# One-core fp32 attention-and-experts block: the router's logits from one packed stationary block of gate parts, and the last batch's logits from four column groups

## The reference, cut to what matters

```python
x = x + tanh(g_xattn[0]) * attention(_layernorm(x), ctx_512, W_k, b_k, ln_gamma, ln_beta)   # softmax of normalised scores
h = _layernorm(x)                        # 2048 tokens x 512
logits = h @ gate_w                      # 2048 x 32: one logit for each token and expert
scores = sigmoid(logits)
sfc = scores + e_bias                    # picks 2 of 4 groups, then 4 of 32 experts
...
routed = einsum('tei,te,eih->th', relu2(einsum('th,ehi->tei', h, Wu)), combine, Wd)
shared = relu2(h @ Wsu) @ Wsd
x = x + tanh(g_ffn[0]) * (routed + shared)
```

## Time and profile before

| | |
|---|---|
| median of 3 runs | 559.65 us |
| lowest and highest run | 558.96 and 562.34 us |
| span of the profiled execution | 550.4 us |
| what lies around the span (lowest run less span) | 8.56 us; to the median it is 9.25 us |
| TensorE matmul busy | 538.5 us (98%) |
| TensorE weight load busy | 440.5 us (80%) |
| VectorE busy | 411.3 us (75%) |
| ScalarE busy | 339.2 us (62%) |
| GpSimd busy | 194.7 us (35%) |
| granted TensorE clock | full (9 of 9 tenths in all 40 slices) |

### The profile page before, as it was taken

One profiled execution on the slowest core, in us unless ns is written; L12 is line 12 of the kernel. 1 busy time (PEld: TensorE's weight loads), 2 busy tenths in 40 slices (PEclk: granted clock), 3 DMA queues, 4 the chain that ended last, 5 costly groups with the idle time before them and its releaser, 6 DMA issues.

```text
span 550.4 us, 11107 instructions
## 1 busy us (share of the span) xinstructions
PE 538.5 (98%) x3079; PEld 440.5 (80%) x3079; DVE 411.3 (75%) x906; ACT 339.2 (62%) x670; POOL 194.7 (35%) x197
## 2 busy tenths in 40 slices
PE   7989999999999999999999999999999999999997
PEld 4547786788688878999999999999998889987553
DVE  5699994494868958656778897777667665756997
ACT  4769573755235855667678787776766766763210
POOL 3110100000000024555656766666666656522000
PEclk9999999999999999999999999999999999999999
DMA  8930102006000006997877988787887778899998
GB/s 316 357 117 23 65 14 76 2 1 229 2 1 0 2 21 197 316 333 247 290 249 254 300 276 261 272 269 263 285 292 265 246 247 262 293 308 386 413 414 302
DMA packets 56393, 116.48 MB, mean 212 GB/s; under 512 B 5493, under 2 KB 24054, under 8 KB 55926
## 3 DMA queue, kind: packets, MB, share of 16 engines
q1 hardware_dynamic: 43200, 72.97, 39.7%
q0 software_dynamic: 12960, 42.48, 21.1%
q10 hardware_dynamic: 150, 0.07, 0.0%
HBM read 85.87 MB, written 29.62 MB: 210 GB/s over the span
## 4 chain that ended last, share of the span: by engine, by line
PE 88%; DVE 7%; ACT 2%; issue 1%; DMA 1%; another core or an unknown queue 0%; ACTq 0%; DVEq 0%; POOLq 0%
PE U L1809 38%; PE D L1809 37%; PE T L2167 6%; PE D L2186 3%; PE T L1809 2%; PE T L1968 1%; DVE X L1135 1%; DVE bst L1140 1%; DVE PS L1123 1%; DVE PS L1117 1%; DMA xg<-h_rows,idx_g 1%; DVE bst L1094 1%; DMA wk<-in_L_xattn_W_k 1%; DVE wsd_lo L1177 0%
## 5 line engine op out<-in xcount | busy, mean ns | idle before, releaser
L621 POOL DMA_INDIRECT xg<-h_rows,idx_g x81 | 88.2, 1089 | 107.9 <-DVE tab L1537 76.7
L628 POOL DMA_INDIRECT y_rows<-yb,idx_s x81 | 92.0, 1136 | 85.1 <-issue 46.9
L1568 DVE TENSOR_TENSOR xgT_lo<-T,xgT_hi 128x512 fp32r<-128x512 f32 x81 | 55.9, 690 | 45.2 <-ACT xgT_hi L923 44.1
L940 ACT ACTIVATE yb<-D 128x512 f32<-128x512 f32 x81 | 48.5, 598 | 53.4 <-PE D L1809 52.1
L1809 PE MATMUL U<-wu_hi,xgT_hi 128*128 x324 | 58.6, 302 | 1.5 <-DVE xgT_lo L1568 1.4
L1809 PE MATMUL D<-wd_hi,eaT_hi 128*128 x162 | 57.3, 435 | 0.1
L923 ACT ACTIVATE xgT_hi<-T 128x512 fp32r<-128x512 f32 x81 | 48.2, 595 | 9.8 <-issue 7.4
L1809 PE MATMUL U<-wu_hi,xgT_lo 128*128 x324 | 51.9, 282 | 0.0
L1809 PE MATMUL U<-wu_lo,xgT_hi 128*128 x324 | 51.7, 281 | 0.0
L1573 DVE SCALAR_TENSOR_TENSOR eact<-U,erel 128x256 f32<-128x256 f32 x81 | 34.0, 419 | 22.5 <-issue 11.7
L1809 PE MATMUL D<-wd_lo,eaT_hi 128*128 x162 | 50.6, 394 | 0.0
(11 more groups left out here) (268 smaller groups left out, 1174.5 us busy)
## 6 DMA issues: line engine op xcount, KB each, us to landing
wu<-in_L_ffn_Wu SPq DMA_DIRECT2D x32, 512.0 KB
wd<-in_L_ffn_Wd SPq DMA_DIRECT2D x32, 512.0 KB
yg<-y_rows SPq DMA_DIRECT2D x18, 512.0 KB, 11.7
out<-X SPq DMA_DIRECT2D x16, 256.0 KB, 5.6
X<-in_x SPq DMA_DIRECT2D x3, 1024.0 KB, 11.0
h_rows<-HR SPq DMA_DIRECT2D x3, 1024.0 KB, 4.3
yg<-y_rows SPq DMA_DIRECT2D x3, 1024.0 KB, 12.9
wsu<-in_L_ffn_Wsu SPq DMA_DIRECT2D x2, 1024.0 KB, 7.3
```

Source lines behind the costliest of these rows:

```text
L621: pool.indirect_dma_start(out=xg[:, u, :], out_offset=None, in_=h_dram[:, :], in_offset=bass.IndirectOffsetOnAxis(ap=idx_g[:, t:t + 1], ax ...
L628: pool.indirect_dma_start(out=y_dram[:, :], in_=yb[:, u, :], in_offset=None, out_offset=bass.IndirectOffsetOnAxis(ap=idx_s[:, t:t + 1], ax ...
L940: ac.activation(yb[:, t % UNROLL, :], D[2 + t % 2][:, :], ACT.Copy)\
L1568: ve.tensor_tensor(xgT_lo[:, t % 2, :, :], T[t % 2][:, :].rearrange("p (h n) -> p h n", h=HB), xgT_hi[:, t % 2, :, :].bitcast(f32), ALU.su ...
```

## The change

For batches 0 to 2 the gates' high part (columns 0 to 31) and low part (columns 32 to 63) stand in one stationary block gate_hl, and `logits_t` runs 8 matmuls: gate_hl by hT_hi and gate_hl by hT_lo. The bank then holds two partial sums on 64 partitions (the product of the two low parts, left out before, is in it). For batch 3 the four fp32 matmuls write four different groups of 32 partitions, each complete in itself, in place of summing into one. ScalarE copies 64 or 128 partitions to lgT, TensorE turns 64 or 128 rows a tile, and VectorE sums the 2 or 4 parts with a tensor_reduce (256 or 512 elements in, 128 out) where it copied. GpSimd writes one block of zeros of 128x256 in place of two of 128x384, and the counts that wait for it go from 22 to 21. In VectorE's list `scaled(1, 3)` moves from behind `low_part(1)` to ahead of `low_part(0)`. The tile `spare` keeps the addresses.

```diff
--- before.py
+++ after.py
@@ -65,7 +65,7 @@
         ebias = sb("ebias", [P, E])
         with ExitStack() as chosen_all:
             wsu_h4 = chosen_all.enter_context(nc.sbuf_tensor("wsu_h4", [P, 2, HB, P], f32r))
-        lgT = sb("lgT", [E, SEQ])
+        lgT = sb("lgT", [P, SEQ])
         LG = sb("LG", [P, NT, E])
         LG2 = LG[:, :, :].rearrange("p t e -> p (t e)")
         bst = sb("bst", [P, 2, TPB, 6])
@@ -129,8 +129,8 @@
             hT_lo = at("hT_lo", [P, 2, HB, SEQ], front, f32r)
             wsu_hi = at("wsu_hi", [P, HB, SI], front, f32r)
             wsd_hi = at("wsd_hi", [P, SB, H], front, f32r)
-            gate_hi = at("gate_hi", [P, HB, P], front, f32r)
-            gate_lo = at("gate_lo", [P, HB, P], front, f32r)
+            gate_hl = at("gate_hl", [P, HB, P], front, f32r)
+            spare = at("spare", [P, HB, P], front)
             act_hi = at("act_hi", [P, A_SLOTS, SEQ], front, f32r)
             with ExitStack() as whole:
                 wsu = at("wsu", [P, HB, SI], whole)
@@ -293,6 +293,10 @@
 
             return U[0 if g else 1]
 
+        def logit_rows(b):
+
+            return HB * E if b == N_BATCH - 1 else 2 * E
+
         def keys_of(b):
 
             return key2[:, b, :] if b < 2 else keyT[:, :]
@@ -581,9 +585,8 @@
             pool.tensor_scalar(part_s[:, :], part_i[:, :], float(P), 0.0, ALU.mult, ALU.add).then_inc(c, 1)
             pool.tensor_copy(tok_f[:, :], tok_i[:, :]).then_inc(c, 1)
             pool.wait_ge(s["pool_c"], 14)
-            same = iota_f[:, E:P].unsqueeze(1).broadcast_to([P, HB, P - E])
-            for part in (gate_hi, gate_lo):
-                pool.tensor_tensor(part[:, :, E:P], same, same, ALU.subtract).then_inc(c, 1)
+            same = iota_f[:, 2 * E:P].unsqueeze(1).broadcast_to([P, HB, P - 2 * E])
+            pool.tensor_tensor(gate_hl[:, :, 2 * E:P], same, same, ALU.subtract).then_inc(c, 1)
             pool.tensor_copy(spare_f[:, :], spare_i[:, :]).then_inc(c, 1)
 
             def roots(j, n):
@@ -598,8 +601,8 @@
             roots(1, 2)
             roots(0, 3)
             pool.wait_ge(s["act_gt"], 1)
-            pool.tensor_tensor(gate_lo[:, :, 0:E], gate[:, :, :],
-                              gate_hi[:, :, 0:E].bitcast(f32), ALU.subtract).then_inc(s["pool_gt"], 1)
+            pool.tensor_tensor(gate_hl[:, :, E:2 * E], gate[:, :, :],
+                              gate_hl[:, :, 0:E].bitcast(f32), ALU.subtract).then_inc(s["pool_gt"], 1)
             roots(1, 4)
             for b in range(2, N_BATCH):
                 roots(0, 2 * b + 1)
@@ -751,7 +754,8 @@
                 ac.wait_ge(s["pe_lgT"], b + 1)
                 if b:
                     ac.wait_ge(s["pe_lg"], b)
-                ac.activation(lgT[:, :], U[1][0:E, :], ACT.Copy).then_inc(s["act_lgT"], 1)
+                n = logit_rows(b)
+                ac.activation(lgT[0:n, :], U[1][0:n, :], ACT.Copy).then_inc(s["act_lgT"], 1)
 
             def high_part(j):
                 ac.wait_ge(d_ws[j], 16)
@@ -803,7 +807,7 @@
             h_t(0, 2)
             h_t(0, 3)
             ac.wait_ge(s["d_gate"], 16 * 2)
-            ac.activation(gate_hi[:, :, 0:E], gate[:, :, :], ACT.Copy).then_inc(s["act_gt"], 1)
+            ac.activation(gate_hl[:, :, 0:E], gate[:, :, :], ACT.Copy).then_inc(s["act_gt"], 1)
             high_part(2)
             exps(1, 0)
             relu2(0)
@@ -1161,7 +1165,9 @@
 
             def logits(b):
                 ve.wait_ge(s["pe_lg"], b + 1)
-                ve.tensor_copy(LG2[:, b * TPB * E:(b + 1) * TPB * E], U[1][:, 0:TPB * E]).then_inc(s["dve_lg"], 1)
+                n = logit_rows(b)
+                parts = U[1][:, 0:TPB * n].rearrange("p (t h e) -> p t e h", t=TPB, e=E)
+                ve.tensor_reduce(LG[:, b * TPB:(b + 1) * TPB, :], parts, AX.X, ALU.add).then_inc(s["dve_lg"], 1)
 
             def high_weights(j):
 
@@ -1200,7 +1206,7 @@
             score_spread(0)
             x_part(1, 0)
             x_part(1, 1)
-            ve.wait_ge(s["pool_c"], 22)
+            ve.wait_ge(s["pool_c"], 21)
             scaled(0, 0)
             scaled(0, 1)
             shifted(0, 0)
@@ -1237,6 +1243,7 @@
             shifted(1, 1)
             low_weights(2)
             low_weights(3)
+            scaled(1, 3)
             low_part(0)
             added(1, 0)
             added(1, 1)
@@ -1245,7 +1252,6 @@
             x2_part(1, 1)
             shifted(1, 2)
             low_part(1)
-            scaled(1, 3)
             added(1, 2)
             shifted(1, 3)
             x2_part(1, 2)
@@ -1974,8 +1980,8 @@
                     pe.wait_ge(s["act_tT"], TPB)
                     pe.wait_ge(s["dve_lg"], b)
                     for h in range(HB):
-                        i_ = mm(U[1][0:E, :].rearrange("p (t n) -> p t n", n=P), gate[:, h, :],
-                                HR[:, :, h * P:(h + 1) * P], h == 0, h == HB - 1)
+                        i_ = mm(U[1][h * E:(h + 1) * E, :].rearrange("p (t n) -> p t n", n=P), gate[:, h, :],
+                                HR[:, :, h * P:(h + 1) * P])
                     i_.then_inc(s["pe_lgT"], 1)
                     return
                 pe.wait_ge(s["act_hT"], TPB * b + TPB)
@@ -1987,17 +1993,17 @@
                 else:
                     pe.wait_ge(s["act_outT"], 4)
                 pe.wait_ge(s["dve_hT"], TPB * b + TPB)
-                gates, hs = (gate_hi, gate_lo), (hT_hi, hT_lo)
-                for a, b_ in ((0, 0), (1, 0), (0, 1)):
+                for part in (hT_hi, hT_lo):
                     for h in range(HB):
-                        i_ = mm(U[1][:, :], gates[a][:, h, :], hs[b_][:, b % 2, h, :], a == b_ == 0 and h == 0,
-                                b_ == 1 and h == HB - 1)
+                        i_ = mm(U[1][:, :], gate_hl[:, h, :], part[:, b % 2, h, :], part is hT_hi and h == 0,
+                                part is hT_lo and h == HB - 1)
                 i_.then_inc(s["pe_lgT"], 1)
 
             def logits(b):
                 pe.wait_ge(s["act_lgT"], b + 1)
+                n = logit_rows(b)
                 for it in range(TPB):
-                    i_ = pe.transpose(U[1][:, it * E:(it + 1) * E], lgT[:, it * P:(it + 1) * P], ident[0:E, 0:E])
+                    i_ = pe.transpose(U[1][:, it * n:(it + 1) * n], lgT[0:n, it * P:(it + 1) * P], ident[0:n, 0:n])
                 i_.then_inc(s["pe_lg"], 1)
 
             ctx_t(0)
@@ -2114,7 +2120,7 @@
             down_shared(12)
             up_shared(15)
             down_shared(13)
-            pe.wait_ge(s["pool_c"], 22)
+            pe.wait_ge(s["pool_c"], 21)
             pe.wait_ge(s["dve_c"], 2)
             pe.wait_ge(s["dve_M"], 2)
             ch = chosen[:, :, :].rearrange("p e t -> p (e t)")
```

## The result

| | kernel before | kernel after |
|---|---|---|
| median | 559.44 us | 556.24 us |
| lowest to highest, 20 runs each | 554.53 to 564.52 us | 553.13 to 559.35 us |
| span of the profiled execution | 550.4 us | 554.3 us |
| first gathered tile on TensorE | 206.52 us | 202.37 us |
| from there to the end of the span | 343.88 us | 351.93 us |

The forecast was 556.5 us. The profiled execution of the changed kernel is nevertheless 3.9 us longer than the one of before. The two lower lines of the table say where that comes from: everything up to the first gathered tile is 4.15 us shorter, and the expert stage of this one execution is 8 us longer. The two halves have to be read apart.

The account below looks back on a forecast made before the run. TensorE was taken as full from 57.3 us on, with the chain through VectorE before that. The terms 0.1 + 1.84 + 1.29 - 0.1 = 3.1 us, off 559.65, gave 556.5 us, range 554.6 to 558.6.

Parts of the forecast that it names:

- Batch 3's products: Batch 3's logits on TensorE: five pass times in place of eight, 1.29 us gained.
- rival 2: Batch 3's logits: all four products run side by side, 2.58 us gained there, 555.2 us in all; chance 0.20.
- Batches 1 and 2: Their logits on TensorE, where it is full: four matmuls fewer in each batch, 1.84 us gained.
- Batch 0 and the move: Up to `ctx_t(3)`: a 0.74 us lead at `down_shared(0)` mostly lost to VectorE's third `h_low`; 0.1 us gained.
- Turning back: TensorE's transposes of the logits: twelve tiles with more rows cost at most 0.2 us, 0.1 taken.
- The sums on VectorE: tensor_reduce in place of the copy: 0.42 and 0.70 us, +0.14 and +0.42, hidden by VectorE's idle time and room.
- The sum over the front: All terms together: 3.1 us gained, with the first gathered tile about 3.1 us earlier.
- What lies around the span: Time outside the profiled span: 9.25 us to the median, taken to stay the same.
- runs as before: Expert stage: starts earlier, with the distance from the first gathered tile to the end the same.
- I am wrong if that distance grows: Test for the expert stage: the distance from the first gathered tile to the end should stay the same.
- rival 3: Expert stage: the weight stream falls behind, 0.85 us a stall, up to 8.8 us slower, 568.5 us; chance 0.05.

Follow-up runs that it names:

- kernel 5: Changed kernel with batch 3's four products in two column groups, alternating 0, 1, 0, 1, two products summed in each; 546.25 us, ratio 0.9936.
- kernel 6: Changed kernel with batch 3's four products in two column groups, in blocks 0, 0, 1, 1, two products summed in each; 546.58 us, ratio 0.9936.
- Kernel 1: Kernel before with only the packing of batches 0 to 2; batch 3 and VectorE's order as before; 552.73 us, ratio 0.9987.
- kernel 3: Changed kernel with `scaled(1, 3)` put back behind `low_part(1)`; 548.04 us, ratio 0.9921.
- Kernel 8: Changed kernel with `scaled(1, 3)` ahead of `low_part(1)`, `shifted(2, 0)` behind batch 1's third `h_low`, and `shifted(2, 1)` ahead of `added(2, 0)`; 545.09 us, ratio 0.9930.
- Kernel 4: Changed kernel with only the counter of two VectorE waits in the expert stage cut to six bits; 549.75 us, ratio 0.9936.
- kernel 9: Kernel before with only the counter of two VectorE waits in the expert stage cut to six bits; 559.86 us, ratio 1.0053.
- kernel 7: Changed kernel with batch 1's eight logit matmuls run eight times over, 56 matmuls more; 558.07 us, ratio 1.0154.
- kernels 1 and 2: The second: kernel before with only batch 3's four products in four column groups, summed by tensor_reduce; 550.11 us, ratio 0.9950.
- 9 to 11: The last two: changed kernel with only the cut wait counter, 551.55 us, ratio 0.9826; the other VectorE order again, 549.42 us, ratio 0.9799.

## Why the prediction was right, and where it was not

The time, 556.5 us, was met by 0.3 us. That it came so close is luck: the front became 4.2 us shorter, not 3.1, and the scatter of the expert stage, or something given back there, hid the surplus.

1. **Batch 3's products: wrong, 1.29 us forecast, 2.56 measured** (3.55 - 0.99). This is the step that failed, and what happened is rival 2, which had a chance of 0.20 beside the forecast's 0.45. The reason given was: "passes start in the order of the list, so the second pass waits for the first. The first pass of the next product can start beside the second of this one, but its own second cannot." Kernels 5 and 6 refute it: by that rule they need 2.25 and 3.1 us, and they took 1.84 and 1.85. A second pass has to wait only within its own group. Four groups of two passes make 2 pass times, two groups of four make 4, one group of eight makes 8. The rule of the Trainium skill (TensorE: Matmul & The Clock Gate, Part 3) that matmuls of different column groups run beside one another held, for products of two passes too. The Trainium skill's other rule in that part, that a weight load overlaps a running matmul only where the row group differs, did not: all eight loads, on the same 128 rows, are through in 0.16 us, while four passes are running. Whether the passes of different groups are brought beside one another when the program is compiled or when it runs, no run here proves. For the second speaks that the two passes that start together stand 13 to 14 ns apart in kernel 6's trace and 6 to 7 in kernel 5's, so TensorE hardly got the same list in both.

2. **Batches 1 and 2: right.** Batch 1's eight matmuls stand in the chain with 1.86 us (1.84 forecast), and from the second four to what follows it is 79.84 - 78.91 = 0.93 us, the 0.92 that was taken off for the missing four. Kernel 1's front is the check: 2 x 0.92 less the 0.12 us by which its `ctx_t(3)` is late (31.94 - 31.82) and less 0.06 for the longer turning back is 1.66, and 1.65 was measured.

3. **Batch 0 and the move: the start right, the sign of the rest wrong, within its bounds.** `down_shared(0)` came at about 56.66 for 56.6. The forecast had the third `h_low` end between 72.57 and 73.05; `ctx_t(3)` came at 73.13, that is 32.01 - 31.82 = 0.19 us late, where 0.1 us early was taken. So the whole lead that the forecast had put at 0.74 us was lost to VectorE, nearly full up to 73 us. The move has no share in the gain: kernel 3 does as well without it, although `down_shared(0)` waits 0.71 us for `scaled` there:

```profile
57.52 0.47 PE L1815 MATMUL D<-wsd_hi,act_hi 128*128 128x512 f32 x1 [0.71 <-DVE PS L1121]
...
73.04 0.62 PE L1838 MATMUL T<-ident,ctx_b 128*128 128x128 f32 x4
```

 Each takes the lead away in one place, TensorE's wait at 57 us or its wait at 73. Kernel 8 shows that a part of the lead was to be had by another order on VectorE, with `scaled(1, 3)` ahead of `low_part(1)` and the third `h_low` ahead of `shifted(2, 0)`: 0.49 us earlier than before at `ctx_t(3)`.

4. **Turning back: right in size.** 0.03 us more for batches 1 and 2 each and 0.08 for batch 3, 0.14 against the 0.1 taken for all.

5. **The sums on VectorE: hidden, as forecast.** 0.41 and 0.68 us. The chosen are ready at 152.60 + 0.72 = 153.32, the first rank matmul starts at about 154.29: 0.97 us of room, where 1.06 had been worked out for the case of all four side by side (155.92 - 154.86). Kernel 4, whose trace has both rank matmuls, has 0.97 as well. Of the room of 2.66 us before, a good third is left.

6. **The sum over the front.** 1.84 + 2.56 - 0.19 less the turning back's 0.14 is 4.07, for 4.21 measured.

7. **What lies around the span: misread.** The prediction kept 9.25 us between span and time. The profiled execution of the changed kernel took 556.18 us for a span of 554.3, so 1.9 lie around it. The execution profiled of before must then have taken about 552.3 us, and the other 7.4 us were that it had been a quick one. It changed nothing in the forecast, as the sum was taken from the median.

8. **The expert stage "runs as before": right on the mean, wrong for a single execution.** It took between 341.2 and 351.9 us, 343.9 and 351.3 with the old front and 341.2 to 351.9 with the new. "I am wrong if that distance grows", the forecast said, and in the result's profile it grew by 8 us; kernel 9 shows that it does so without the change. That is a loss of rival 3's kind without rival 3's cause. What goes with it is ScalarE going on late (0 to 15.2 us in all) at a semaphore that TensorE raises. What holds it was not tested.

That leaves 4.2 us of front against 2.7 (1.6 to 3.8) in the time. On the quietest occasion, where before's 13 runs lay within 2.3 us (kernels 5 to 8), the medians follow the fronts within 0.4 us: 3.28 us for 3.13 (kernel 5), 2.95 for 3.09 (kernel 6), 4.44 for 4.79 (kernel 8), -8.54 for -8.54 (kernel 7). There the kernel before, by its median less 1.9 us and its front, had an expert stage of about 549.5 - 1.9 - 206.5 = 341.1 us, as short as the 341.2 to 342.2 of these four; that is an estimate, as it wasn't profiled on this occasion. On kernel 4's occasion the changed kernel gained 3.25 for 4.19, without the move 4.96 for 4.28, and kernels 1 and 2 gained 0.27 for 1.65 and 2.89 for 2.60. I take it that the front's gain arrives and the expert stage's scatter covers it; that up to 1 us is given back in the expert stage is not excluded.

The version with the other order is the best of those run. Its front is 0.5 to 0.6 us shorter than the changed kernel's in both executions; its ratio beside the changed kernel's, 0.9799 [0.9756, 0.9842] to 0.9826 [0.9781, 0.9870], does not separate them.

## What to carry to other kernels

Where small products use few columns of TensorE, give each a column group of its own, even if it makes an engine that has room add up four parts: four fp32 products fell from 3.55 to 0.99 us for 0.4 us more on VectorE. When TensorE gets ahead, look at who is late next within the following 20 us; here an engine at 15.2 of 15.7 us took the whole lead of batch 0, and another order of its steps gave some two thirds of it back. And where one stage scatters by 10 us from one execution to the next, compare the kernels by marks ahead of it, and look at several executions each, before a span is read as a result.

## What the runs showed of the hardware

- Column groups of fp32 products keep their order within a group only: eight passes in one, two and four groups took 3.55, 1.84 or 1.85, and 0.99 or 1.00 us.
- Passes in one group followed each other every 0.43 us, though each is shown as 592 ns or more; the four that start together in the changed kernel are shown with up to 617.
- The same expert stage at full clock took 341.2 to 351.9 us from one execution to another, with 0 to 15.2 us of ScalarE's waits that the profile calls `remote`, longer waits with longer stages. Kernels 1 to 4 and 9 to 11 ran on one chip: 342.4 to 351.3 us there, and the kernel before had medians of 553.0 and 559.7 us on its two occasions on that chip. Kernels 5 to 8 ran on another, with 341.2 to 342.2 us and none of these waits; whether the chip or the hour makes that difference, no run here shows.
